# A language-model layer on one core: LSTM cell work placed one or two gate units later, halves kept in pairs, and each step's front begun six units early

## The chip, the core and the metric

One core of a Trainium2 chip. Its engines run their own instruction streams and meet at semaphores: TensorE (PE, matmuls; PEld, its weight loads), VectorE (DVE), ScalarE (ACT), GpSimd (POOL) and SyncE (SP, which here only issues DMAs; ScalarE's queue, ACTq, issues some as well). The metric is the device time of one execution, in microseconds (us).

## What is computed

`x` holds 16 rows of 512 token numbers. For each row:

```
h = concat(emb_table[x], stft_magnitudes(one_hot(x)) @ proj_w + proj_b)    # 512 x 128
h = h + attention(layernorm(h))      # 8 heads of 16; 64 summary tokens, window of 17 keys for the other 448
h = h + moe(layernorm(h))            # 8 experts, top 2
```

The experts of `moe` are LSTMs. The 16 rows are the time steps of the recurrence, the 512 tokens its batch; both choices (K = 2) of all 8 experts carry their own state:

```
gates = xt @ Wi + h @ Wh + b;  i, f, g, o = split(gates, 4)
c = sigmoid(f) * c + sigmoid(i) * tanh(g);  h = sigmoid(o) * tanh(c);  y = h @ Wo + bo
```

with `xt` the token times its 0/1 mask for this choice and expert, and the output the sum over choices of mask x router weight x y.

## The kernel before

Activations lie transposed, 128 features on the partitions and tokens along the free axis; both choices stand side by side, so a gate is 128 x 1024.

**Gate units.** A step s is 32 gate units t = 0..31; expert e = t // 4, gate g = t % 4 in the order I, G, F, O. A unit (`unit_gate`, matmuls on L506) is 12 matmuls of 512 columns: input and hidden state, each split into a high and a low 16-bit half, three products of halves, two choices. It writes one of two PSUM slots, which ScalarE empties with a tanh (`gate_tanh`, L655). Step 0 has no hidden state and no F gate: 24 units of 6 matmuls.

**Cell work.** On VectorE: `masked_input` (L985), `input_part` (L1007), `cell` (L1013, L1017), `hidden` (L992), `hidden_lo` (L997), `chosen` (L1028, L1032: the state of the chosen token's expert, weighted). On ScalarE: `cell_tanh` (L662) and `split_hi` (L666). On TensorE `unit_y` (L512) adds the expert's output. Before the change, counted in units: `cell` at g = 2 of its own expert, `cell_tanh` at g = 3; `hidden` and `split_hi` at g = 0 of the next expert, `hidden_lo` at g = 1, `chosen` at g = 2; `unit_y` at g = 0 of the expert after that.

**The front.** All that a step needs ahead of its LSTM (ids, one-hot, embedding, layernorm, attention, second layernorm, routing, masks) is called the front. The front of step s + 1 is spread by hand over the units of step s: each engine calls `front(t, s + 1)` at unit t, and four tables (`SP_AT`, `PE_AT`, `ACT_AT`, `DVE_AT`) say at which t each piece stands on each engine. Engines run strictly in the order written. Front 0 stands alone ahead of step 0. Pieces that the prediction names, with their lines: embedding matmuls (PE, L420), first transposes (L427), query, key and value (L432), summary scores (L436), window scores (L441, L447: 84 matmuls of 32 columns with block-diagonal weights `diag`), feature scores (L453), values (L459, the same shape), projection (L465, L466), second transposes (L471), logits (L477), mask transposes (L483); on VectorE one-hot (L779), moments (L763 to L789), normalising (L795), value windows (L824), probability transpose (L882); on GpSimd the inverse root (L1105).

**DMAs.** The weights `diag` are filled by four block copies from `pr` (queries, issued by SP) and again by four from `vwin` (values, issued on ScalarE's queue, L619). Routing masks go to DRAM (`mask_scratch`, `mw_scratch`) at t = 28 and come back broadcast: `masks` two for each step's first experts at t = 29, 30, then one per expert; `rowk1` and `roww` at g = 3, each waiting for an earlier `chosen`.

Of the kernel before, what the change touches and what calls it, by code (L numbers as in the profile page):

```python
# [5 lines left out]
def lm_tower_kernel(nc, x_ids, frame_ids, emb_table, proj_w, proj_b, w_qkv, b_qkv, w_out, b_out,  # L6
# [20 lines left out]
    P = 128  # L27
# [43 lines left out]
    with ctx:  # L71
# [16 lines left out]
        tmp = sb("tmp", [P, 7, K * SEQ])  # L88
# [6 lines left out]
        z32 = sb("z32", [P, SEQ])  # L95
# [23 lines left out]
        diag = sb("diag", [P, 2, NBLK, NG, 2 * DH], f16)  # L119
# [14 lines left out]
        qz = pr[:, :].bitcast(f16).rearrange("p (v j c q) -> p v j c q", v=2, j=NBLK, c=2)  # L134
# [3 lines left out]
        vw16 = vwin[:, :].bitcast(f16).rearrange("p (v j d) -> p v j d", v=2, j=NBLK)  # L138
        vhl = ew[:, 0:TF + 2 * PAD].bitcast(f16).rearrange("p (v t) -> p v t", v=2)
# [31 lines left out]
        def gate_at(gate, e):  # L171

            return {I: e % 2, G: 2 + e % 2, F: 4, O: 5 + e % 2}[gate]

        TANH_C = gate_at(F, 0)
# [3 lines left out]
        diag_flat = diag[:, :, :, :, :].rearrange("p v j g d -> p (v j g d)")  # L179
        onehot64 = diag_flat[0:NFFT, 2 * VOCAB * NBJ:3 * VOCAB * NBJ]  # L180
        mag = diag_flat.bitcast(f32)[0:NFREQ, 0:VOCAB * NBJ]
# [100 lines left out]
        def _(sp):  # L282
# [19 lines left out]
            def front(t, b):  # L302
                if t == SP_AT["ids"]:
                    sp_ids(b)
                if t == SP_AT["qbd"]:
# [3 lines left out]
                    for g in range(NG):  # L309
                        load(diag[32 * g:32 * g + 32, :, :, g, :].rearrange("p v j d -> p (v j) d"),  # L310
                             qz[32 * g:32 * g + 32, :, :, :, :].rearrange("p v j c q -> p (v j) (c q)"), S["qbd"])
# [47 lines left out]
            def step(s, par, first, last):  # L359
                for t in range(NG * E):  # L360
                    e, g = t // NG, t % NG
                    if t == 9 and not first:
# [811 lines left out]
```

## Time and profile before

| | |
|---|---|
| median of 3 runs | 1915.93 us (1915.46 to 1918.11) |
| the profiled execution's own time | 1918.11 us, its span 1916.3 us |
| TensorE busy | 1729.1 us (90% of the span) |
| VectorE busy | 1559.5 us (81%) |
| ScalarE busy | 991.9 us (52%) |
| GpSimd busy | 65.2 us (3%) |
| chain that ended last, by engine | PE 40%, DVE 33%, DMA 8%, issue 7%, ACT 5%, ACTq 4% |
| gate matmuls (L506) | 5904, 1451.7 us |

A timeline gives for each instruction its start, its duration, engine, line, operation, what it writes and reads, and in brackets how long its engine was idle before it and what ended the wait. Instructions of one form in a row are merged ("x6"). Matmuls are pipelined, so that one is shown longer than it keeps the next from starting.

### The profile page before, as it was taken

Reading aid. Unit: us, or ns where it says so; the run is one execution under the profiler, and the core shown is the slowest. Engines: PE = TensorE matmul, PEld = TensorE weight load, DVE = VectorE, ACT = ScalarE, POOL = GpSimd, SP = SyncE. Lnnn points to the kernel's source line nnn. Section 1 sums busy time; section 2 is a strip of 40 time slices with the busy share of each in tenths; the row PEclk is TensorE's granted clock in tenths of the full one; section 3 lists DMA queues with packets and bytes.
Section 4 is the critical chain, followed back from the end, with each engine's and each line's share of the span. In section 5 each row is a group of like instructions: output and inputs, shape, how many; then the busy total and the mean of one; then the engine's idle time right before and its main releaser. Section 6 shows DMA issues by size and latency. Waiting matters only on the chain.

```text
span 1916.3 us, 25885 instructions
## 1 busy us (share of the span) xinstructions
PE 1729.1 (90%) x9898; PEld 837.6 (44%) x9898; DVE 1559.5 (81%) x2433; ACT 991.9 (52%) x1114; POOL 65.2 (3%) x42
## 2 busy tenths in 40 slices
PE   3457799999999999999999999999999999999998
PEld 2223344444444444444444444444444444444443
DVE  2649698897988889798898988889898888979865
ACT  3234554646555555645545455455555555564544
POOL 1000000000000000000000000000000000000000
PEclk9668899999999999999999999999999999999999
DMA  3113241413314132232313224151331413223221
GB/s 114 20 41 74 57 67 46 77 37 67 63 49 74 39 70 52 52 70 51 67 45 69 51 57 67 44 80 37 63 66 46 76 37 71 53 50 67 55 61 36
DMA packets 318594, 110.95 MB, mean 58 GB/s; under 512 B 240331, under 2 KB 299581, under 8 KB 318471
## 3 DMA queue, kind: packets, MB, share of 16 engines
q1 hardware_dynamic: 202758, 101.96, 23.9%
q10 hardware_dynamic: 115712, 7.34, 3.8%
q8 instruction: 78, 1.28, 0.3%
q14 instruction: 46, 0.37, 0.1%
HBM read 89.84 MB, written 4.74 MB: 49 GB/s over the span
## 4 chain that ended last, share of the span: by engine, by line
PE 40%; DVE 33%; DMA 8%; issue 7%; ACT 5%; ACTq 4%; SPq 1%; POOL 0%; DVEq 0%
PE gates L506 25%; ACTq L619 4%; DVE C L1017 4%; DVE tmp L1007 4%; DMA masks<-mask_scratch 3%; DVE tmp L1013 3%; DMA prod<-in_x_ids 3%; DVE xm L985 3%; PE yp L512 3%; DVE Hs L997 3%; DVE tmp L1028 3%; DVE xn L795 2%; PE FA L447 2%; ACT tmp L655 2%; PE FA L459 2%
## 5 line engine op out<-in xcount | busy, mean ns | idle before, releaser
L655 ACT ACTIVATE tmp<-gates,bias_sb 128x1024 f32<-128x1024 f32 x504 | 557.5, 1109 | 558.6 <-PE gates L506 496.1
L506 PE MATMUL gates<-xm,wi_sb 128*128 128x512 f16 x3024 | 747.3, 384 | 46.2 <-ACT tmp L655 31.0
L506 PE MATMUL gates<-Hs,wh_sb 128*128 128x512 f16 x2880 | 704.4, 381 | 0.0
L506 PEld LDWEIGHTS gates<-xm,wi_sb 128*128 128x128 f16 x3024 | 290.3, 99 | 435.3 <-issue 105.1
L506 PEld LDWEIGHTS gates<-Hs,wh_sb 128*128 128x128 f16 x2880 | 283.2, 98 | 344.3 <-issue 8.0
L662 ACT ACTIVATE tmp<-C 128x1024 f32<-128x1024 f32 x128 | 135.2, 1057 | 226.4 <-DVE C L1017 223.2
L992 DVE SCALAR_TENSOR_TENSOR tmp<-tmp 128x1024 f32<-128x1024 f32 x128 | 155.9, 1218 | 71.8 <-ACT tmp L662 71.8
L1007 DVE SCALAR_TENSOR_TENSOR tmp<-tmp 128x1024 f32<-128x1024 f32 x120 | 144.9, 1208 | 46.4 <-ACT tmp L655 44.9
L985 DVE TENSOR_TENSOR xm<-xs,masks 128x2048 f16<-128x2048 f16 x128 | 155.2, 1212 | 32.7 <-DMA masks<-mask_scratch 32.7
L997 DVE SCALAR_TENSOR_TENSOR Hs<-tmp,Hs 128x1024 f16<-128x1024 f32 x120 | 146.4, 1220 | 37.7 <-ACT Hs L666 36.7
L1013 DVE SCALAR_TENSOR_TENSOR tmp<-tmp,C 128x1024 f32<-128x1024 f32 x120 | 146.4, 1220 | 14.4 <-ACT tmp L655 14.0
L1017 DVE SCALAR_TENSOR_TENSOR C<-tmp 128x1024 f32<-128x1024 f32 x120 | 147.0, 1225 | 4.1
L666 ACT ACTIVATE Hs<-tmp 128x1024 f16<-128x1024 f32 x120 | 126.5, 1055 | 31.2 <-DVE tmp L992 30.7
L512 PE MATMUL yp<-z,wo_sb 128*128 128x512 f32 x256 | 134.9, 609 | 8.2 <-DVE z L1032 8.2
L1105 POOL TENSOR_TENSOR rstd<-veps,mhalf 128x4 f32<-128x4 f32 x32 | 61.6, 1926 | 1682.6 <-DVE veps L922 1114.8
L1032 DVE TENSOR_TENSOR z<-tmp,roww 128x512 f32<-128x512 f32 x128 | 88.6, 692 | 13.6 <-DVE tmp L1028 0.5
L1028 DVE COPY_PREDICATED tmp<-rowk,tmp 128x512 f32<-128x512 uint16 x128 | 93.0, 727 | 0.1
L512 PEld LDWEIGHTS yp<-z,wo_sb 128*128 128x128 f32 x256 | 48.0, 194 | 38.8 <-issue 12.2
L459 PE MATMUL FA<-vwin,diag 128*128 128x32 f16 x1344 | 36.3, 177 | 7.4 <-DVE vwin L882 7.4
L447 PEld LDWEIGHTS FA<-xn,diag 128*128 128x128 f16 x1344 | 38.2, 97 | 8.1 <-issue 5.5
L459 PEld LDWEIGHTS FA<-vwin,diag 128*128 128x128 f16 x1344 | 36.0, 96 | 12.5 <-DVE vwin L882 9.2
L447 PE MATMUL FA<-xn,diag 128*128 128x32 f16 x1344 | 39.1, 178 | 0.0
(155 smaller groups left out, 1218.9 us busy)
## 6 DMA issues: line engine op xcount, KB each, us to landing
masks<-mask_scratch SPq DMA_DIRECT2D x128, 256.0 KB, 5.0
roww<-mw_scratch SPq DMA_DIRECT2D x128, 256.0 KB, 4.0
rowk<-mask_scratch SPq DMA_DIRECT2D x128, 128.0 KB, 3.0
diag<-pr SPq DMA_DIRECT2D x64, 112.0 KB, 4.3
diag<-vwin ACTq DMA_DIRECT2D x64, 112.0 KB, 4.8
out_dram<-h SPq DMA_DIRECT2D x16, 256.0 KB, 3.7
C<-in_wi SPq DMA_DIRECT2D x1, 2048.0 KB, 10.9
C<-in_wh SPq DMA_DIRECT2D x1, 2048.0 KB, 15.6
```

What stands on the lines that cost most here:

```text
L506: last = mm(gates[:, slot, k * SEQ:(k + 1) * SEQ], w, v, start=(i < K), stop=(i >= len(seq) - K))
L512: mm(yp[:, :], wo_sb[:, e, :], z32[:, :], start=False, stop=(e == E - 1)).then_inc(s_y, 1)
L655: A(tmp[:, gate_at(gate, e), :], gates[:, (n - 1) % 2, :], ACT.Tanh, bias=bias_sb[:, e, gate:gate + 1], scale=UNSCALE).then_inc(s_tanh, 1)
L662: A(tmp[:, TANH_C, :], C[:, e, :], ACT.Tanh, scale=0.5).then_inc(s_tc, 1)
L666: A(Hs[:, e, HI, :], tmp[:, gate_at(O, e), :], ACT.Copy, scale=V_SCALE).then_inc(s_hhi, 1)
L985: TT(xm[:, e % 2, :, :, :], xv, mv_, ALU.mult).then_inc(s_xm, 1)
L992: STT(out=at, in0=at, scalar=1.0, in1=tmp[:, TANH_C, :], op0=ALU.add, op1=ALU.mult).then_inc(s_h, 1)
L997: STT(out=Hs[:, e, LO, :], in0=tmp[:, gate_at(O, e), :], scalar=V_SCALE, in1=Hs[:, e, HI, :], op0=ALU.mult, op1=ALU.subtract).then_inc(s_h ...
L1007: STT(out=at_i, in0=at_i, scalar=1.0, in1=at_g, op0=ALU.add, op1=ALU.mult).then_inc(s_u, 1)
L1013: STT(out=at_f, in0=at_f, scalar=1.0, in1=C[:, e, :], op0=ALU.add, op1=ALU.mult).then_inc(s_v, 1)
L1017: STT(out=C[:, e, :], in0=at_f, scalar=0.5, in1=tmp[:, gate_at(I, e), :], op0=ALU.mult, op1=ALU.add).then_inc(s_c, 1)
L1028: V.copy_predicated(at[:, 0:SEQ], rowk1[:, e % 2, :].bitcast(u16), at[:, SEQ:2 * SEQ]).then_inc(s_sel, 1)
```

## The change

- The tables place each piece of the front again, most of them two units earlier, and the first ones at negative positions -6 to -1, which are units 26 to 31 of the step ahead (`EARLY = 6`, `run_front`). For front 1 these positions come at unit 0 of step 0.
- `cell` moves to g = 0 of the next expert, `cell_tanh` too, `hidden` to its g = 1, `split_hi` to g = 2, `hidden_lo` and `chosen` to g = 3, `unit_y` to g = 1 of the expert after that. F's tanh has two buffers (`tmp` 8 slots instead of 7), and the cell's tanh goes into F's. `chosen` writes into the free half of O's buffer instead of `z32`.
- The two 16-bit halves of queries (`qz`), values (`vp16`) and `diag` lie next to each other in pairs instead of in two planes. The value windows are one 32-bit transpose instead of two 16-bit ones, the block copies move 32-bit pairs (runs of 128 B instead of 64 B), and the weights of window scores and values are read with a step of two elements.
- The embedding matmuls also wait for the mask copies of the front before.

```diff
-    SP_AT = dict(ids=0, qbd=6, rows=28)
-    PE_AT = dict(emb=1, xT=3, qkv=4, summary=7, window=8, feature=14, values=18, proj=21, x2T=23,
-                 logits=24, maskT=27)
-    ACT_AT = dict(h=1, xT=3, qkv=4, split=5, summary=9, window=11, vz=9, pr_hi=15, feature=16, x2T=23,
-                  choice=25, maskT=27)
-    DVE_AT = dict(onehot=0, moments=1, xn=2, pw=5, q_lo=5, kv_lo=6, v_win=7, w_max=8, s_max=9, s_sub=10, w_sum=11,
-                  w_out=12, s_sum=13, s_norm=14, f_max=15, p_lo=16, p_T=16, f_sum=17, f_part=18, attn=19,
-                  moments2=21, xn2=22, x_lo=24, choice1=25, choice2=25, weights=26)
+    SP_AT = dict(ids=-6, qbd=3, rows=28)
+    PE_AT = dict(emb=-3, xT=0, qkv=1, summary=4, window=6, feature=12, values=16, proj=18, x2T=22,
+                 logits=23, maskT=27)
+    ACT_AT = dict(h=-3, xT=0, qkv=1, split=2, summary=6, window=9, vz=7, pr_hi=13, feature=14, x2T=22,
+                  choice=24, maskT=27)
+    DVE_AT = dict(onehot=-4, moments=-2, xn=-1, pw=2, q_lo=2, kv_lo=3, v_win=4, w_max=5, s_max=7, s_sub=8, w_sum=9,
+                  w_out=10, s_sum=11, s_norm=12, f_max=13, p_lo=14, p_T=15, f_sum=16, f_part=16, attn=17,
+                  moments2=19, xn2=20, x_lo=23, choice1=24, choice2=24, weights=25)
+    EARLY = 6
...
+        def run_front(front, t, s):
+            if s == 0 and t == 0:
+                for u in range(-EARLY, 0):
+                    front(u, 1)
+            if s + 1 < STEPS:
+                front(t, s + 1)
+            if s + 2 < STEPS and t >= NG * E - EARLY:
+                front(t - NG * E, s + 2)
...
                 if t == PE_AT["emb"]:
+                    if not is_zero(b):
+                        pe.wait_ge(S["mrow"], b)
+                        pe.wait_ge(S["wT"], b)
...
-                                last = mm(FA[:, r, jj * KB:(jj + 1) * KB], diag[:, qv, j, :, :].rearrange("p g d -> p (g d)"),
+                                last = mm(FA[:, r, jj * KB:(jj + 1) * KB], diag16[:, j, :, qv],
...
-                        act.dma_start(diag[32 * g:32 * g + 32, :, :, g, :].rearrange("p v j d -> p (v j) d"),
-                                      vw16[32 * g:32 * g + 32, :, :, :].rearrange("p v j d -> p (v j) d")) \
+                        act.dma_start(diag[32 * g:32 * g + 32, :, g, :], vwj[32 * g:32 * g + 32, :, :]) \
...
-                    for v in (HI, LO):
-                        own = vhl[:, v, :]
-                        win = bass.AP(tensor=own.tensor, offset=own.offset, ap=[list(own.ap[0]), [QB, NBLK], [1, KB]])
-                        last = V.transpose(vw16[:, v, :, :], win)
-                    last.then_inc(S["vwin"], 1)
+                    win = bass.AP(tensor=vp.tensor, offset=vp.offset, ap=[list(vp.ap[0]), [QB, NBLK], [1, KB]])
+                    V.transpose(vwj, win).then_inc(S["vwin"], 1)
...
             def gate_tanh(s, e, g, first):
-                if gate == F and m >= 1:
-                    act.wait_ge(s_h, m)
+                if gate == F and m >= 2:
+                    act.wait_ge(s_h, m - 1)
                 elif gate == O and m >= 2:
-                    act.wait_ge(s_z, m - 1)
+                    act.wait_ge(s_y, m - 1)
...
             def step(s, par, first, last):          # ScalarE
-                    if g == 3:
-                        cell_tanh(s, e)
+                    if g == 0 and e:
+                        cell_tanh(s, e - 1)
...
-                    if g == 0 and e and not last:
+                    if g == 2 and e and not last:
                         split_hi(s, e - 1)
...
             def step(s, par, first, last):          # VectorE, its order within a unit
+                    if g == 0 and e and not first:
+                        cell(s, e - 1)
                     if g == 1 and e < E - 1:
                         masked_input(s, e + 1, par, first and e == 0)
                     if t == XM_AT and not last:
                         masked_input(s + 1, 0, 1 - par, False)
+                    if g == 3 and e and not last:
+                        hidden_lo(s, e - 1)
+                    if g == 3 and e:
                         chosen(s, e - 1)
                     if t == YADD_AT and not first:
                         add_y(s - 1, 1 - par)
+                    run_front(lambda u, b: front(u, b, b % 2), t, s)
+                    if g == 1 and e:
+                        hidden(s, e - 1)
+                    if g == 2:
                         input_part(s, e, first)
-                    if g == 2 and not first:
-                        cell(s, e)
```

## Rows read from the trace of the kernel before

**Rows 1.** Stretches, length; busy PE, PEld, DVE, ACT, POOL; clock, DMA share, GB/s.

```profile
900.96:1014.89 113.93, 108.22 (x630) 52.44 (x631) 98.06 (x153) 62.06 (x70) 3.82 (x2) 1.00 0.29 58
...
216.71:1812.41 1595.70, 1521.80 (x8821) 737.44 (x8822) 1370.76 (x2127) 862.35 (x965) 53.50 (x28) 0.99 0.29 58
```

**Rows 2.** Timeline of TensorE, step 7; in brackets idle before, and its releaser.

```profile
907.75 1.16 PE L420 MATMUL FB<-table,rows 41*128 41x128 f32 x8 [0.59 <-DVE rows L779]
908.84 1.47 PE L506 MATMUL gates<-xm,wi_sb 128*128 128x512 f16 x6
910.14 1.46 PE L506 MATMUL gates<-Hs,wh_sb 128*128 128x512 f16 x6
...
915.01 0.66 PE L427 MATMUL FB<-ident,xn 128*128 128x128 f32 x4 [0.82 <-DVE xn L795]
...
946.47 1.47 PE L506 MATMUL gates<-xm,wi_sb 128*128 128x512 f16 x6 [0.62 <-ACT tmp L655]
...
966.12 1.47 PE L506 MATMUL gates<-xm,wi_sb 128*128 128x512 f16 x6 [1.47 <-ACT tmp L655]
...
1002.61 0.63 PE L483 MATMUL FB<-ident,pr 128*72 128x128 f32 x4 [1.15 <-DVE pr L973]
...
1014.89 1.46 PE L506 MATMUL gates<-xm,wi_sb 128*128 128x512 f16 x6 [0.44 <-issue]
```

**Rows 3.** Timeline of ScalarE and its queue (ACTq), same step.

```profile
942.40 2.80 ACTq L619 DMA_DIRECT2D diag<-vwin  x2
...
962.96 1.06 ACT L662 ACTIVATE tmp<-C 128x1024 f32<-128x1024 f32 x1 [3.19 <-DVE C L1017]
...
964.98 1.09 ACT L655 ACTIVATE tmp<-gates,bias_sb 128x1024 f32<-128x1024 f32 x1
965.96 1.05 ACT L666 ACTIVATE Hs<-tmp 128x1024 f16<-128x1024 f32 x1
```

**Rows 4.** Timeline of VectorE, same step, a stretch without waits.

```profile
953.30 1.22 DVE L985 TENSOR_TENSOR xm<-xs,masks 128x2048 f16<-128x2048 f16 x1
954.43 1.22 DVE L997 SCALAR_TENSOR_TENSOR Hs<-tmp,Hs 128x1024 f16<-128x1024 f32 x1
...
958.00 0.73 DVE L1028 COPY_PREDICATED tmp<-rowk,tmp 128x512 f32<-128x512 uint16 x1
...
959.45 1.09 DVE L875 TENSOR_TENSOR vwin<-pr,wred 128x896 f32<-128x896 f32 x1
...
966.41 1.11 DVE L882 STREAM_TRANSPOSE vwin<-pr 128x896 f32<-128x896 f32 x1
967.45 1.18 DVE L985 TENSOR_TENSOR xm<-xs,masks 128x2048 f16<-128x2048 f16 x1
```

**Rows 5.** Timeline of all engines and queues, end of the same step.

```profile
1007.15 0.28 SPq L284 DMA_DIRECT2D mw_scratch<-rows  x1
...
1013.57 1.22 DVE L985 TENSOR_TENSOR xm<-xs,masks 128x2048 f16<-128x2048 f16 x1 [1.88 <-DMA masks<-mask_scratch]
```

**Rows 6.** Timeline of VectorE, same step, instructions of the front.

```profile
909.89 0.85 DVE L763 BATCH_NORM_STATS2 stats<-h_sb 128x6 f32<-128x128 f32 x4
...
911.27 1.22 DVE L1007 SCALAR_TENSOR_TENSOR tmp<-tmp 128x1024 f32<-128x1024 f32 x1
...
913.85 1.11 DVE L795 TENSOR_SCALAR xn<-h_sb,mv,rstd 128x128 f32<-128x128 f32 x4
...
932.28 2.10 DVE L824 STREAM_TRANSPOSE vwin<-ew 128x896 f16<-128x896 f16 x2
```

**Rows 7.** Timeline of TensorE, same step, groups without a wait ahead.

```profile
955.11 0.92 PE L453 MATMUL FB<-prod,hones 128*128 128x448 f32 x2
...
961.04 1.02 PE L512 MATMUL yp<-z,wo_sb 128*128 128x512 f32 x2
...
968.72 2.25 PE L459 MATMUL FA<-vwin,diag 128*128 128x32 f16 x84
```

**Rows 8.** Timeline of TensorE, step 0.

```profile
131.93 0.79 PE L427 MATMUL FB<-ident,xn 128*128 128x128 f32 x4 [3.95 <-DVE xn L795]
```

More of the change, by code:

```diff
@@ L361, in step @@
                     e, g = t // NG, t % NG
-                    if t == 9 and not first:
+                    if t == 10 and not first:
                         store(s - 1, 1 - par)
-                    if not last:
-                        front(t, s + 1)
+                    run_front(front, t, s)
                     if g == 1 and e < E - 2:
@@ L373, in step @@
                         rows_in(s + 1, 0)
-            for t in range(NG * E):
+            for t in range(-EARLY, NG * E):
                 front(t, 0)
@@ L540, in step @@
                         y_back(s - 1)
-                    if not last:
-                        front(t, s + 1)
+                    run_front(front, t, s)
             pe.wait_ge(s_const, 16 * len(consts))
@@ L546, in _ @@
             pe.wait_ge(s_prep, 4)
-            for t in range(NG * E):
+            for t in range(-EARLY, NG * E):
                 front(t, 0)
@@ L678, in step @@
                         y_out(s - 1)
-                    if g == 0 and e and not last:
+                    if g == 0 and e:
+                        cell_tanh(s, e - 1)
+                    elif g == 0 and not first:
+                        cell_tanh(s - 1, E - 1)
+                    if g == 2 and e and not last:
                         split_hi(s, e - 1)
-                    elif g == 0 and not e and not first:
+                    elif g == 2 and not e and not first:
                         split_hi(s - 1, E - 1)
-                    if g == 3:
-                        cell_tanh(s, e)
-                    if not last:
-                        front(t, s + 1)
+                    run_front(front, t, s)
             par_of = lambda b: PAR[0]
@@ L706, in _ @@
             split_w_hi(wh_st, wh_sb, 0.5, s_wh_load)
-            for t in range(NG * E):
+            for t in range(-EARLY, NG * E):
                 front(t, 0)
@@ L991, in hidden @@
                 at = tmp[:, gate_at(O, e), :]
-                STT(out=at, in0=at, scalar=1.0, in1=tmp[:, TANH_C, :],
+                STT(out=at, in0=at, scalar=1.0, in1=tmp[:, gate_at(F, e), :],
                     op0=ALU.add, op1=ALU.mult).then_inc(s_h, 1)
@@ L1061, in step @@
                         add_y(s - 1, 1 - par)
-                    if not last:
-                        front(t, s + 1, 1 - par)
-                    if g == 1:
+                    run_front(lambda u, b: front(u, b, b % 2), t, s)
+                    if g == 1 and e:
+                        hidden(s, e - 1)
+                    elif g == 1 and not first:
+                        hidden(s - 1, E - 1)
+                    if g == 2:
                         input_part(s, e, first)
-                    if g == 2 and not first:
-                        cell(s, e)
             dve.wait_ge(s_zero, 1)
-            for t in range(NG * E):
+            for t in range(-EARLY, NG * E):
                 front(t, 0, 0)
@@ L1081, in _ @@
             run_steps(step)
+            cell(STEPS - 1, E - 1)
             hidden(STEPS - 1, E - 1)
@@ L1107, in step @@
             def step(s, par, first, last):
-                if not last:
-                    for t in range(NG * E):
-                        front(t, s + 1)
+                for t in range(NG * E):
+                    run_front(front, t, s)
             pool.wait_ge(s_zero, 1)
-            for t in range(NG * E):
+            for t in range(-EARLY, NG * E):
                 front(t, 0)
```

76 lines of the change are left out of this document (36 added, 40 removed).

## Prediction

> **What bounds the kernel now.** I read the totals by engine first, then the busy sums by step, then TensorE's timeline through one step, and last the timelines of the engines that it waits for. A step is taken from the first gate matmul of one step to that of the next. Fourteen steps (1 to 14) take 1595.70 us, 113.98 each, at a clock of 0.99, which is the 2.4 GHz level; in step 7 VectorE is busy 98.06 of 113.93 us [rows 1]. So neither engine is full. TensorE is the nearer: its matmuls are shown 0.16 us longer than they hold the next one off (half a gate unit is shown as 1.47 us and the next half starts 1.30 us later [rows 2]), and its real idle time is the bracket in a row plus 0.16. Step 7 has seven waits over 0.4 us; their brackets are 0.59, 0.82, 0.62, 1.47, 0.62, 1.15 and 0.44 us (six of the rows stand in [rows 2]), 5.7 in sum, 6.8 with 0.16 each. The rest, 107.1 us, is matmuls back to back: that is the floor of a step, and 6.8 to 6.9 us a step (14 x 6.9 = 97 us) is all that another order can win.
>
> What each wait hangs on: embedding matmuls on the one-hot rows (0.59), the first transposes on the normalised input (0.82), gate units on a tanh of ScalarE (0.62 and 1.47), the second transposes (0.62), the mask transposes (1.15), the step's first gate unit on the masked input (0.44) [rows 2]. Behind the 0.62 one stands ScalarE's queue issuing the value copies, of which two took 2.80 us [rows 3]; behind the 1.47 one ScalarE waited 3.19 us for VectorE's new cell state before it could go on to the next gates [rows 3].
>
> **The change part by part.** Positions are gate units t of a step, four to an expert.
>
> *Cell work later.* Nothing is removed; cell, hidden, its halves and the chosen row move one or two positions later, and F's tanh gets a second buffer. ScalarE's tanh of the cell now comes after the next expert's first gate. From G's tanh to that point are three units, 7.8 us; VectorE must fit in input part, low half, chosen row and cell: 1.14 + 1.14 + 1.45 + 2.4 = 6.1 us (an operation over 1024 elements lets the next begin 1.13 to 1.14 us later, the chosen row's two take 1.45, and the cell is two long ones, the second waiting for the first) [rows 4], and the gates' two PSUM slots give ScalarE 1.9 us more (two units, 5.2, less the cell's tanh, the gate tanh ahead of it and the one behind, 1.1 each [rows 3]). So 3.6 us of front work fits in the last two positions of an expert. By the ops' durations the experts have 0 to 3.2 us there; only the last has more, and there TensorE waits in any case (below). The 1.47 wait and the 0.62 behind the value copies go: there the queue's four issues now come at t = 7, before units with 1.9 us of bias and output matmuls among them. I take these as won, worth 1.63 + 0.78.
>
> *Front begun six units early.* Ids are asked for at t = 26 of the step before the last one; SP's queue reaches it right after the row loads of t = 23, five units (13 us) before the one-hot, so the ids wait goes (0.75). The embedding's new wait for the mask copies is for copies made two units earlier, at no cost while those stand. The second transposes (t = 22, statistics at 19) and mask transposes (t = 27, weights at 25) get two units and one unit more and lose their waits (0.78 and 1.31). The mask copies no longer queue behind the cell's tanh, so the masked input is ready before the step's first unit (0.59).
>
> *What is late next, first place: the first transposes.* The moments at t = 30 stand on VectorE's queue behind the next step's masked input, and that waits for a load of masks. Counted from the end of unit 27: VectorE ends chosen row at +2.3 (ScalarE's tanh and high half of unit 26 end at -0.4, then 1.14 + 1.45), SP's row loads that wait for it take 0.8, the mask rows go out at +3.4, and from there to the masked input's start are 6.42 us in the row, 1013.57 - 1007.15 [rows 5]: +9.8. Then masked input 1.14, moments 1.38, input part 1.14, low half 1.14, chosen row 1.45, normalising 1.11 [rows 4, 6]: +17.2. The 1.9 us of GpSimd between the moments and the normalising lie beside the three in the middle. TensorE comes there after the mask transposes 0.47, five units 12.95, output matmuls 0.86 and embedding 1.09 [rows 2, 7]: +15.4. Wait: 1.8 us, where 0.98 was.
>
> *Second place: the values.* They need the transposed probabilities, now at t = 15 for t = 16. VectorE is held at t = 11 for the high half, 2.25 us after unit 10 (a tanh 0.2 after the unit, 0.98 to the next start, 1.05 [rows 3]). From there it is never free: the stretch from the masked input at 953.30 to 967.45, fifteen instructions back to back, is the same list less one low half and one chosen row [rows 4]: 14.15 + 1.14 + 1.45 = 16.7. TensorE needs six units 15.54, feature scores 0.76, output 0.86 [rows 7] = 17.2. Wait: 2.25 + 16.7 + 0.05 - 17.2 = 1.9 us, where none was shown.
>
> *Halves in pairs.* Two 16-bit transposes of 2.10 us together [rows 6] become one of 32 bits on the same 896 elements; the existing one of that form takes 1.11 [rows 4], so VectorE gains 1.0 us a step, beside the path but for the first front. The block copies move runs of twice the length and half as many; at worst they cost what they do (2.80 us for two [rows 3]), at best half. The strided writes of ScalarE may cost 0.1 to 0.3 us a step; all but the first front's lie where both engines have room. The diagonal weights are now read with a gap between elements. Today 84 such loads with their 32-column matmuls take 2.25 - 0.16 = 2.1 us, 25 ns a pair [rows 7]. Bounds: 25 ns as now, or, if a load gets only one column in the time in which a 512-column matmul streams one (216 ns / 512 x 128), 54 ns. I take 25, since the second matmul group already streams paired halves at the price of the first; that is the moving side, though, so 54 stays as a rival.
>
> The rule that bears on this: the Trainium skill, "TensorE: Matmul & The Clock Gate", section on weight-path perf modes, says that the fast load takes 128 columns of a type other than fp32, packed or strided, but also that it reads 32 bits at a time, two 16-bit weights. By its first half the pair costs what it does, and the sum would be 1872. By its second a gap could waste half of each read; an estimate from that page, at twice the time for a pair, is 15 x 168 x 25 ns = 63 us more, 1935. The trace of before has no such load, so it shows neither.
>
> *Ends of the run.* In step 0 the early six positions of front 1 fall behind its first unit. There the chain is bare: today the transposes come at 131.93 after a wait of 3.95 us [rows 8]. They now start some 2.6 us sooner by the clock but with two units fewer behind them (5.2 us); I take +2, bounds -3 and +7. The first front, a bare chain, loses 1.0 of transpose and perhaps as much of copying: -2. The tail keeps its chain (the last cell still starts when F's tanh is there): 0.
>
> **Sum.** A step: 107.1 + 1.8 + 1.9 = 110.8 to 110.9 against 113.98, 3.1 less; 14 steps: -43.5; ends 0. The profiled execution took 1918.11 us with a span of 1916.3, so 1874.6; the median of the runs, 1915.93, gives 1872.4. I say 1872.
>
> **The rivals.**
> *All waits gone.* If the mask load lands a microsecond or two sooner and VectorE's list is shorter than counted, a step falls to 107.1 and the run to 1915.9 - 97 = 1819. For it: both waits left are under 2 us. Against: they are two separate chains, each counted from rows. Chance 0.10, most of it only part of the way.
> *The waits move, and nothing is won.* VectorE with 97 us of work and some 1.5 us of gaps in 111 is 89% full; if it reaches each cell more than the 3.6 us late, ScalarE holds the gates again. It takes 0.4 us at each of eight experts to eat the 3.1: 1916. For it: no spare time from t = 11 to 16. Against: elsewhere it is held for ScalarE's high half, so it has time. Chance 0.15, of it 0.06 still faster, 0.05 within 0.2% and 0.04 slower.
> *Slower: the spaced weights.* At 54 ns a pair, 168 pairs a step cost 4.9 us more, all on TensorE, whose floor they raise, in the 15 fronts that lie inside steps: 15 x 4.9 = 73, so 1872 + 73 = 1945. It decides from 3.1 us / 168 = 18 ns on, 43 ns a pair. Chance 0.11.
>
> **The numbers.** The forecast has 0.64; its own range is 1855 to 1893 (1.3 us a step either way, and 5 us at the ends). Faster by over 0.2% (about what a measurement of this kernel can tell from no change): 0.64 + 0.10 + 0.06 = 0.80. Within: 0.05. Slower: 0.04 + 0.11 = 0.15. The range goes to 1848 below (part of "all gone") and 1908 above (part of "nothing won"), leaving out the spaced weights and the rest.
>
> **What the profile after would show.** Right: steps of about 111 us; no wait over 0.4 us at the embedding, second transposes, mask transposes and step's first unit; one of 1.6 to 1.8 (bracket) at the first transposes, released by the normalising, and one like it at the values, released by the 32-bit transpose; gate units with no wait for ScalarE; groups of 42 diagonal matmuls in 1.05 us as today. Wrong, if those groups take over 1.8 us, if the cell's tanh shows waits of several microseconds followed by idle gates, or if masks land later than 10 us after unit 27.

## The result and the profile after

The changed kernel takes 1947.24 us (median of 4 runs, 1944.00 to 1949.43) against 1917.02 for the kernel before in the same runs: ratio 1.0156, 95% interval 1.0137 to 1.0174. It is slower; the forecast of 1872 and its range are missed. The profiled execution took 1947.46 us, its span is 1945.7.

The page of the changed kernel: totals of the engines, and the value copies with their us from issue to landing.

```profile
PE 1740.4 (89%) x9898; PEld 850.1 (44%) x9898; DVE 1548.8 (80%) x2417; ACT 998.0 (51%) x1114; POOL 63.4 (3%) x42
...
diag<-vwin ACTq DMA_DIRECT2D x64, 112.0 KB, 7.5
```

Stretches of the changed kernel (columns as in [rows 1]): step 8, steps 1 to 14, step 0.

```profile
1026.01:1142.11 116.10, 109.16 (x630) 53.38 (x631) 97.39 (x152) 62.00 (x70) 3.82 (x2) 0.99 0.26 57
212.56:1841.81 1629.25, 1533.98 (x8812) 748.77 (x8813) 1360.63 (x2112) 870.38 (x965) 53.52 (x28) 0.98 0.26 57
...
116.42:212.56 96.14, 67.59 (x390) 32.55 (x391) 71.45 (x128) 50.32 (x59) 2.01 (x2) 0.82 0.29 63
```

Steps 1 to 14 take 116.37 us each where they took 113.98 [rows 1]: 33.5 us in all. The start is shorter, step 0 beginning at 116.42 instead of 120.16, and step 0 itself takes 96.14. TensorE's timeline in step 8 and at its end:

```profile
1026.01 1.46 PE L522 MATMUL gates<-xm,wi_sb 128*128 128x512 f16 x6 [0.60 <-issue]
...
1032.21 0.90 PE L443 MATMUL FB<-ident,xn 128*128 128x128 f32 x4 [3.45 <-DVE xn L811]
1032.90 2.77 PE L522 MATMUL gates<-xm,wi_sb 128*128 128x512 f16 x6
1035.46 1.68 PE L522 MATMUL gates<-Hs,wh_sb 128*128 128x512 f16 x6
...
1055.71 1.21 PE L463 MATMUL FA<-xn,diag 128*128 128x32 f16 x42
...
1069.20 1.04 PE L522 MATMUL gates<-xm,wi_sb 128*128 128x512 f16 x4 [1.16 <-ACT tmp L669]
...
1091.05 1.11 PE L475 MATMUL FA<-vwin,diag 128*128 128x32 f16 x38 [1.93 <-DVE vwin L895]
...
1113.65 0.60 PE L487 MATMUL FB<-ident,xn 128*128 128x128 f32 x4
...
1128.70 0.60 PE L499 MATMUL FB<-ident,pr 128*72 128x128 f32 x4
...
1135.27 1.16 PE L436 MATMUL FB<-table,rows 41*128 41x128 f32 x8
...
1142.11 1.46 PE L522 MATMUL gates<-xm,wi_sb 128*128 128x512 f16 x6 [0.40 <-issue]
```

Of the waits of [rows 2], those at the embedding, the second transposes and the mask transposes are gone (1135.27, 1113.65, 1128.70), and so is the 1.47 behind the cell's tanh. In their place stand 3.45 us at the first transposes, 1.16 at the gate unit after t = 9 (0 to 1.5 over the steps), 1.93 at the values and 0.40 (0.4 to 1.8 over the steps) at the step's first unit. And half a gate unit, which starts the next half 1.30 us later [rows 2], takes 2.56 right behind the first transposes (1032.90 to 1035.46): the clock is granted at 1.2 GHz for 3.41 us.

The clock's record counts 19 such stretches of 3.41 us begun in steps 1 to 14, where before had 5, and 4.1 us of a longer one that began in step 0. Of the 19, 13 begin behind the first transposes, 4 behind the values and 2 behind the wait after t = 9. If half of each stretch is lost, a step loses 2.46 us to the clock, and 0.61 before. By this count a step at full clock takes 113.91, and 113.37 before: the rest grew by 0.5 us a step, the clock's loss by 1.9. The experiments are read in the same three numbers.

The count is an upper bound for the clock, because other engines catch up while TensorE is slow, and waits that follow get shorter (in E9 below the gate unit after t = 9 waits 0.36 us in step 9, which has a stretch, and 1.11 in step 10, which has none). TensorE's timeline gives another split: its idle time (each bracket over 0.15 us plus 0.16) is 7.4 us a step, 6.3 before, and its matmuls, at whichever clock, fill 108.9, and 107.7 before. **So waits and clock share the 2.4 us a step about evenly: 1.15 and 1.25.**

### The profile page after: what moved, and what is told of

The parts are those of the page before. It is cut to its first block, busy times and chain, and to the rows that moved or that the text cites. A ratio compares the mean times of both kernels' runs of the same rounds, so it can differ in the third digit from the quotient of the medians.

```text
span 1945.7 us, 25741 instructions
## 1 busy us (share of the span) xinstructions
PE 1740.4 (89%) x9898; PEld 850.1 (44%) x9898; DVE 1548.8 (80%) x2417; ACT 998.0 (51%) x1114; POOL 63.4 (3%) x42
## 4 chain that ended last, share of the span: by engine, by line
PE 56%; DVE 25%; DMA 7%; ACTq 5%; issue 4%; ACT 3%; SPq 1%; POOL 0%; DVEq 0%
PE gates L522 40%; ACTq L634 5%; DVE Hs L1010 3%; DMA masks<-mask_scratch 3%; PE yp L528 3%; DVE xm L998 3%; DMA mw_scratch<-rows 2%; DVE tmp L1020 2%; DVE tmp L1041 2%; PE FA L475 2%; DVE tmp L1005 2%; PE FA L463 2%; PE FA L448 1%; PE FB L482 1%; ACT tmp L669 1%
## 5 line engine op out<-in xcount | busy, mean ns | idle before, releaser
L522 PE MATMUL gates<-xm,wi_sb 128*128 128x512 f16 x3024 | 763.5, 390 | 41.2 <-issue 15.1
L522 PEld LDWEIGHTS gates<-xm,wi_sb 128*128 128x128 f16 x3024 | 295.1, 100 | 444.8 <-issue 129.6
L528 PE MATMUL yp<-tmp,wo_sb 128*128 128x512 f32 x256 | 134.0, 605 | 5.9 <-DVE tmp L1043 5.9
L1043 DVE TENSOR_TENSOR tmp<-tmp,roww 128x512 f32<-128x512 f32 x128 | 88.6, 692 | 4.4
L817 DVE TENSOR_TENSOR prod<-qT,kw 128x64 f32<-128x64 f32 x16 | 4.4, 275 | 83.9 <-ACT kf L613 83.9
L443 PE MATMUL FB<-ident,xn 128*128 128x128 f32 x64 | 16.0, 397 | 60.7 <-DVE xn L811 60.7
L528 PEld LDWEIGHTS yp<-tmp,wo_sb 128*128 128x128 f32 x256 | 47.8, 193 | 36.0 <-issue 12.7
```

The source lines that it names most:

```text
L522: last = mm(gates[:, slot, k * SEQ:(k + 1) * SEQ], w, v, start=(i < K), stop=(i >= len(seq) - K))
L528: mm(yp[:, :], wo_sb[:, e, :], chosen_at(e), start=False, stop=(e == E - 1)).then_inc(s_y, 1)
```

## The experiments

"Step" is the mean length of steps 1 to 14, "clock" half of the time that it spent at the half clock, "rest" the difference; "clock" is an upper bound, so that "rest" is somewhat too low where "clock" is large. Step, clock and rest are those of the profiled execution. Medians stand against 1917 to 1920 us of the kernel before on the same chip.

| kernel | us | ratio, 95% interval | step | clock | rest |
|---|---|---|---|---|---|
| before | 1917.0 | | 113.98 | 0.61 | 113.37 |
| after | 1947.2 | 1.0156 (1.0137 to 1.0174) | 116.37 | 2.46 | 113.91 |
| E1 mask rows at 27 | 1890.2 | 0.9851 (0.9833 to 0.9869) | 112.57 | 1.58 | 110.99 |
| E2 store at 14 | 1960.5 | 1.0198 (1.0175 to 1.0220) | 117.35 | 3.29 | 114.06 |
| E3 pairs alone | 1896.0 | 0.9875 (0.9861 to 0.9890) | 112.86 | 0.37 | 112.49 |
| E4 later cell alone | 1997.7 | 1.0394 (1.0367 to 1.0422) | 119.24 | 5.40 | 113.84 |
| E5 early front alone | 1949.3 | 1.0161 (1.0146 to 1.0176) | 115.54 | 3.69 | 111.85 |
| E6 value copies at 6 | 1944.7 | 1.0131 (1.0116 to 1.0146) | 116.28 | 3.61 | 112.67 |
| E7 rows 27, values 17 | 1847.7 | 0.9625 (0.9609 to 0.9642) | 109.50 | 0.37 | 109.14 |
| E8 E7 and copies at 6 | 1840.3 | 0.9593 (0.9579 to 0.9608) | 108.95 | 0.85 | 108.09 |
| E9 values 17 alone | 1917.7 | 0.9993 (0.9981 to 1.0004) | 114.18 | 1.96 | 112.22 |
| E10 moments first | 1931.0 | 1.0062 (1.0047 to 1.0077) | 115.18 | 2.71 | 112.47 |
| E11 E8, moments first | 1831.7 | 0.9546 (0.9532 to 0.9560) | 108.43 | 0.69 | 107.74 |
| E12 E4, rows at 27 | 1942.7 | 1.0132 (1.0102 to 1.0161) | 115.32 | 3.53 | 111.79 |
| E13 waits filled | 1943.5 | 1.0114 (1.0093 to 1.0135) | 115.90 | 1.10 | 114.79 |
| E14 E6, filled | 1925.3 | 1.0034 (1.0021 to 1.0046) | 114.88 | 1.08 | 113.80 |
| E15 E11, filled | 1834.1 | 0.9553 (0.9539 to 0.9567) | 108.61 | 0.81 | 107.80 |
| E16 E11, one bias matmul | 1816.8 | 0.9465 (0.9448 to 0.9482) | 107.50 | 0.12 | 107.38 |
| E17 E13, one bias matmul | 1921.5 | 1.0004 (0.9992 to 1.0017) | 114.09 | 0.26 | 113.83 |

### The parts of the change, each alone (E3, E4, E5)

E3 is the kernel before with the pairs: `diag`, `qz`, `vp16` interleaved, one 32-bit transpose, 32-bit copies, weights read with a step. E4 is the kernel before with the cell work of the changed one. E5 is the kernel before with the changed tables and `run_front`.

> The kernel before with the halves in pairs and nothing else. Theory (pairs cost nothing, weights with a step of two load as fast): 84 diagonal matmuls in 2.1 us as before, value copies issued in 3 us instead of 4.4, the 0.6 to 0.8 us wait for ScalarE behind them gone; 1900 to 1912 us. Rival (pair runs slow the copies on ScalarE's queue): four issues of 6 us or more, 1925 us or above.

> The kernel before with the cell work later (second buffer of F, orders of ScalarE, VectorE and TensorE within an expert) and nothing else: the old tables, planes instead of pairs. Theory (the later cell takes the wait of 1.47 us for ScalarE away and brings none): 1.5 us a step less, 1890 to 1900 us. Rival (work moved past the front's pieces makes the front late, and the waits at transposes grow by as much): 1912 us or more.

> The kernel before with the new tables, the front begun six units early and the embedding's new wait, and nothing else: old cell order, planes instead of pairs. Theory (the late mask load is made by the chosen row and SP's row loads being later, so with the old cell order the mask rows go out without row loads ahead of them): write to masked input in 6.5 us as before, wait at the first transposes 1 us or less, total 1885 to 1905 us. Rival (the early front itself makes the chain masks, moments, normalising too long): first transposes wait over 3 us and the clock falls behind it, 1925 us or more.

The pairs win 24 us, more than was expected: the value copies issue in 3.0 us instead of 4.4, landing after 3.1 instead of 4.8, and the start is 3.6 us shorter. ScalarE's writes with a gap take longer, 0.77 us instead of 0.66 for each of two and 0.73 instead of 0.59 for one, 0.36 us a step. From the page of E3:

```profile
diag<-vwin ACTq DMA_DIRECT2D x64, 112.0 KB, 3.1
```

The other two lose, so both rivals had the time right, but neither had the place. In E5 the mask load is issued 1.45 us after the second write, as before, and the masked input starts 5.9 to 6.6 us after that write: this half of the theory came true. The rest falls by 1.5 us a step (1.7 to 2.3 us of wait at the first transposes, 3.08 at the values, at most 1.0 elsewhere), but the clock takes 3.1 more, nearly all of it behind the values and behind the projection, and step 0 takes 104.6 instead of 96.6. In E4 the waits grow not at transposes but in three other places, at the embedding (1.1 to 3.3), the values (1.76) and the step's first unit (1.8 to 3.4), and the clock takes 4.8 more.

### The mask rows behind the row loads (E1, E12)

```diff
-    SP_AT = dict(ids=-6, qbd=3, rows=28)
+    SP_AT = dict(ids=-6, qbd=3, rows=27)
```

> The changed kernel with the mask rows written to DRAM at t = 27, ahead of SP's two row loads, instead of at t = 28 behind them. Theory (the mask load is late because its writes stand behind the row loads, and take 3.4 us there instead of 1.5): the masked input of the next step starts 2.5 to 3 us sooner, the wait at the first transposes falls from 3.45 to under 1.2 us, the wait at the step's first gate unit goes, and TensorE's clock stays at its upper level there; 1865 to 1885 us. Rival 1 (VectorE's own list between masked input and normalising is too long whatever the load does): the 3.45 stays, about 1947 us. Rival 2 (the clock falls at any wait there): the wait shrinks but the clock share stays 0.985 in every step, about 1895 to 1900 us.

> The kernel before with the later cell work alone (1997.7), and the mask rows written at t = 27 instead of 28. Theory A: the later chosen row holds SP's row loads back and the mask rows stand behind them, which makes the wait of 2 to 3.4 us at each step's first unit; it falls under 1 us, 25 to 40 us less in all, 1955 to 1975, the waits at embedding and values staying. Rival: the step's first unit waits for the cell work itself, and moving the rows does nothing: 1990 to 2000.

The changed kernel between unit 27 and the transposes that wait, ScalarE, VectorE and SP's queue:

```profile
1130.51 0.59 ACT L656 ACTIVATE rows<-FB 8x512 f32<-8x512 f32 x1
1130.93 0.69 DVE L1043 TENSOR_TENSOR tmp<-tmp,roww 128x512 f32<-128x512 f32 x1
...
1131.65 0.35 SPq L362 DMA_DIRECT2D rowk<-mask_scratch  x1
...
1132.04 0.42 SPq L364 DMA_DIRECT2D roww<-mw_scratch  x1
1132.59 0.35 SPq L298 DMA_DIRECT2D mask_scratch<-ew  x1
...
1132.98 0.32 SPq L298 DMA_DIRECT2D mw_scratch<-rows  x1
...
1136.34 1.19 SPq L352 DMA_DIRECT2D masks<-mask_scratch  x2
...
1140.79 1.22 DVE L998 TENSOR_TENSOR xm<-xs,masks 128x2048 f16<-128x2048 f16 x1 [4.42 <-DMA masks<-mask_scratch]
...
1147.15 1.11 DVE L811 TENSOR_SCALAR xn<-h_sb,mv,rstd 128x128 f32<-128x128 f32 x4
```

The rows are ready at 1131.1, yet go out at 1132.59 and 1132.98, behind two row loads that had to wait for the chosen row (1131.6). SP issues the mask load only once both writes have landed, 3.36 us after the second. The same place in E1:

```profile
1098.95 0.31 SPq L298 DMA_DIRECT2D mask_scratch<-ew  x1
...
1099.56 0.27 SPq L298 DMA_DIRECT2D mw_scratch<-rows  x1
1100.10 0.35 SPq L362 DMA_DIRECT2D rowk<-mask_scratch  x1
1100.49 0.42 SPq L364 DMA_DIRECT2D roww<-mw_scratch  x1
1101.03 1.17 SPq L352 DMA_DIRECT2D masks<-mask_scratch  x2
...
1105.99 1.23 DVE L998 TENSOR_TENSOR xm<-xs,masks 128x2048 f16<-128x2048 f16 x1 [1.18 <-DMA masks<-mask_scratch]
```

The second write has landed by 1101.03, after 1.47 us at most. So a write right behind two loads lands 1.9 us later than one ahead of them. The Trainium skill, "DMA: Bandwidth & Descriptors", section on queues, rings and completion order, says that a DMA's semaphore is counted only after every earlier write of the same DMA engine, across its queues. The trace agrees as far as it goes: all of the writes' semaphore counts but one come at 1135.54 to 1136.32, those of the two loads until 1136.16. It does not tell whether the writes' data, too, stood behind the loads' in the queue. In E1 the wait at the first transposes is 0.8 to 2.0 us, the one at the step's first unit is gone, and 57 us come off, 5 less than the least that was expected. No low stretch is left behind the first transposes from step 2 on, but one now follows the values in 12 of 14 steps, where 4 had one in the changed kernel with the same pause of 1.93 us. E12 shows the same on the cell work alone: the wait at the first unit goes, and 55 us with it, more than expected, up to half of it clock. In E4 these rows made that wait:

```profile
1166.33 0.32 SPq L360 DMA_DIRECT2D rowk<-mask_scratch  x1
...
1167.23 0.38 SPq L296 DMA_DIRECT2D mask_scratch<-ew  x1
...
1170.97 0.90 SPq L350 DMA_DIRECT2D masks<-mask_scratch  x2
...
1175.51 1.23 DVE L997 TENSOR_TENSOR xm<-xs,masks 128x2048 f16<-128x2048 f16 x1 [4.46 <-DMA masks<-mask_scratch]
1176.84 1.58 PE L517 MATMUL gates<-xm,wi_sb 128*128 128x512 f16 x6 [2.47 <-issue]
```

### The value copies on ScalarE's queue (E2, E6)

The changed kernel, ScalarE and both queues at t = 9 and 10:

```profile
1060.19 0.32 SPq L362 DMA_DIRECT2D rowk<-mask_scratch  x1
...
1060.86 7.07 ACTq L634 DMA_DIRECT2D diag<-vwin  x4
1061.09 0.38 SPq L352 DMA_DIRECT2D masks<-mask_scratch  x1
1061.56 0.41 SPq L370 DMA_DIRECT2D out_dram<-h  x1
...
1068.03 1.11 ACT L669 ACTIVATE tmp<-gates,bias_sb 128x1024 f32<-128x1024 f32 x1 [6.12 <-issue]
```

Four issues hold ScalarE for 7.07 us and the next tanh with it. E2 moves the store away from them (`if t == 14 and not first:` instead of 10), E6 the copies away from the loads (`vz=6` instead of 7 in `ACT_AT`).

> The changed kernel with the output store at t = 14 instead of t = 10, so that its 256 KB do not meet the value block copies of ScalarE's queue. Theory A (the store slows the four issues from 4.4 to 6.7 us and so holds the gate tanh): the four issues take 4.5 us or less, the wait of 0.5 to 1.5 us at the gate unit after t = 9 goes, 1931 to 1937 us. Theory B (the mask and row loads that leave at the same moment do it): issues stay at 6 us or more, 1945 to 1949 us. Theory C (runs of 128 bytes do it): as B, and the kernel before with pairs shows it too.

> The changed kernel with the value block copies at t = 6 of ScalarE's queue instead of t = 7, so that they are issued before SP's mask and row loads of the first chosen row leave. Theory (these loads, at the same moment, stretch the four issues to 6.7 us): four issues in 3 to 3.5 us, as with pairs alone, and no wait of 0.5 to 1.5 us at the gate unit behind t = 9; 1930 to 1936 us. Rival (the copies are slow after any late position, or the wait has another releaser): issues over 6 us or the wait stays, 1945 us or more.

E2 is 13 us slower instead of faster, of which the clock column has 12, and the issues still take 5.9 to 7.3 us. In E6 they start 1.9 us before SP's loads instead of among them:

```profile
1059.22 3.31 ACTq L634 DMA_DIRECT2D diag<-vwin  x4
1061.16 0.32 SPq L362 DMA_DIRECT2D rowk<-mask_scratch  x1
```

Over the steps from 2 on they take 3.0 to 3.4 us. So here it is the loads, not the store. (In E5, with the old 64 B runs, the copies leave 0.5 us behind the store and 2.6 behind a mask load and take 5.2 to 7.0, so that a store may do it too; no run separates the two there.) The wait after t = 9 is gone and the rest falls by 1.24 us a step, which is the 17 us that were expected; the clock takes 1.15 more, with a stretch behind both pauses in nearly every step, and 2.5 us are left of it.

### The values a unit later (E7, E8, E9)

```diff
-    PE_AT = dict(emb=-3, xT=0, qkv=1, summary=4, window=6, feature=12, values=16, proj=18, x2T=22,
+    PE_AT = dict(emb=-3, xT=0, qkv=1, summary=4, window=6, feature=12, values=17, proj=19, x2T=22,
...
-                  w_out=10, s_sum=11, s_norm=12, f_max=13, p_lo=14, p_T=15, f_sum=16, f_part=16, attn=17,
-                  moments2=19, xn2=20, x_lo=23, choice1=24, choice2=24, weights=25)
+                  w_out=10, s_sum=11, s_norm=12, f_max=13, p_lo=14, p_T=15, f_sum=16, f_part=16, attn=18,
+                  moments2=20, xn2=21, x_lo=23, choice1=24, choice2=24, weights=25)
```

E9 has this edit alone, E7 with E1's, E8 with E1's and E6's.

> The changed kernel with mask rows written at t = 27 and with the values one unit later (TensorE t = 17, what follows them one later as well). Theory (the wait of 1.93 us at the values is VectorE's list from t = 11 to 15, and the 3.4 us at the clock's lower level that follow it in every step are its consequence): the wait falls under 0.4 us, the lower level goes from the steps, 3.6 us a step less than with the rows alone: 1838 to 1850 us. Rival 1 (the clock falls without the wait too): 1862 us. Rival 2 (the wait moves on to the attention sum and projection): 1880 us or more.

> The changed kernel with all three: mask rows at t = 27, value copies at t = 6, values at t = 17. If the three causes are separate, their gains add: about 1 us a step less than with the first and third alone, 1825 to 1838 us. If one wait merely takes the place of another, it ends within 5 us of the kernel without the copies moved.

> The changed kernel with only the values and what follows them one unit later, the mask rows left at t = 28. Both theories: the wait of 1.93 us at the values goes (14 x 2.1 = 29 us), the one of 3.45 at the first transposes stays. Theory A, the long wait by itself brings TensorE's clock down for 3.41 us in each step: clock about 0.985, time 1903 to 1920. Rival, the clock only falls because a step has two long waits: clock 0.995 or more, time 1898 or less.

E7 and E9 came out as expected (E9 by theory A), E8 2 us above: against E7 its rest falls by 1.05 us a step and the clock takes 0.48 back. Alone the edit wins 30 us, beside E1's 43, because there the fall of the clock behind the values goes with it (17 us in the clock column, 7 in E9). But E9 also shows the limit of theory A, for the clock falls behind the first transposes in 9 of 14 steps only. Steps 9 and 10 of the same run, their stretches first, then TensorE in them:

```profile
1129.12:1242.84 113.72, 108.77 (x631) 53.54 (x632) 97.41 (x152) 62.53 (x70) 3.83 (x2) 0.98 0.26 58
1242.84:1355.54 112.70, 107.43 (x630) 52.80 (x631) 97.39 (x152) 61.59 (x70) 3.83 (x2) 1.00 0.29 58
```

```profile
1135.32 1.12 PE L443 MATMUL FB<-ident,xn 128*128 128x128 f32 x4 [3.45 <-DVE xn L811]
1136.23 2.29 PE L522 MATMUL gates<-xm,wi_sb 128*128 128x512 f16 x5
```

```profile
1249.04 0.66 PE L443 MATMUL FB<-ident,xn 128*128 128x128 f32 x4 [3.46 <-DVE xn L811]
1249.54 1.46 PE L522 MATMUL gates<-xm,wi_sb 128*128 128x512 f16 x6
```

The same pause of 3.45 us brings the clock down in one step and not in the next.

### The order of moments and masked input (E10, E11)

```diff
-                    if t == XM_AT and not last:
-                        masked_input(s + 1, 0, 1 - par, False)
...
                     run_front(lambda u, b: front(u, b, b % 2), t, s)
+                    if t == XM_AT and not last:
+                        masked_input(s + 1, 0, 1 - par, False)
```

> The changed kernel with one order reversed: at t = 30 VectorE does the early front's moments ahead of the next step's masked input instead of behind it. Theory A, the moments' 1.38 us fit in the 4.4 us in which VectorE waits for the mask load, so that the normalising and the first transposes come 1.4 us earlier and nothing else later: wait 3.45 to about 2.0, 1926 to 1930, or 1903 to 1915 if the clock no longer falls there. Rival, the step's start then waits for the masked input instead: 1942 to 1950.

> The kernel with mask rows at t = 27, value copies at 6 and values at 17 (1840.3), with the moments ahead of the masked input. Theory A: the last wait, 0.83 to 1.8 us at the first transposes, goes, 14 x 1.25 = 17 us, or 27 with the clock's low stretches: 1812 to 1825. Rival: the mask load now lands before the moments are over, so the masked input comes late for the step's first unit, and the wait only moves: 1835 to 1842.

In E10 the wait at the first transposes is 2.06 us in every step, 1.4 less, and the masked input starts only 0.3 us later after the second write (8.3 us on the mean instead of 8.1): theory A's mechanism, and 16 us instead of 17 to 21. The clock still falls, in most steps twice. E11 wins 9 us, half of the 17: 0.82 us of the wait stay in every step, now behind ScalarE's high half, then VectorE's low half, chosen row and normalising, a chain that the moments are no part of.

### Pauses filled with matmuls (E13, E14, E15)

```diff
+                    for _i in range(0 if is_zero(b) else 15):
+                        mm(FB[:, :], wi_sb[:, 0, HI, 0:P], wi_sb[:, 0, LO, 0:4 * P], start=True, stop=True)
...
+                    pe.wait_ge(S["df"], b1)
+                    for _i in range(0 if is_zero(b) else 8):
+                        mm(FB[:, :], wi_sb[:, 0, HI, 0:P], wi_sb[:, 0, LO, 0:4 * P], start=True, stop=True)
```

The 15 stand ahead of the wait at the first transposes, the 8 ahead of the one at the values. E13 is the changed kernel with both, E14 is E6 with both, E15 is E11 with 4 at the first place alone.

> The changed kernel with extra matmuls of 512 columns whose results nobody reads, 15 (3.2 us) ahead of the wait at the first transposes and 8 (1.7 us) ahead of the one at the values. They fill the pauses and take no work away, so the waits' time stays spent. Theory A, TensorE's pauses bring its clock down and that costs 2.46 us a step: the clock in steps 1 to 14 stays at 1.00, and the time falls by about 14 x 2.4 = 34 us: 1910 to 1920. Rival, the clock falls for another reason (the work itself, its 16-bit columns): it falls as before or more, 1943 to 1955.

> The changed kernel with the value copies issued at unit 6 (1944.7) and the same fillers in both pauses. Theory A, the 1.2 us a step that the earlier copies won there were lost to a second fall of the clock in each step (3.61 us a step in all): 1944.7 - 14 x 3.6 = 1894, 1890 to 1902. Rival, the earlier copies win nothing: same as the kernel with fillers alone, 1910 to 1920, or 1943 and more if fillers do nothing.

> The fastest kernel so far (1831.7: mask rows at 27, value copies at 6, values at 17, moments ahead of the masked input), with 4 fillers (0.86 us) ahead of its one wait of 0.82 us. Theory A: the clock's four low stretches in steps 1 to 14 (0.69 us a step) go, 1822 to 1828. Rival: they follow the chain of small matmuls later in the step and stay, 1830 to 1836.

TensorE in E13, step 8:

```profile
1033.05 3.40 PE L442 MATMUL FB<-wi_sb 128*128 128x512 f16 x15
1036.68 0.66 PE L445 MATMUL FB<-ident,xn 128*128 128x128 f32 x4 [0.22 <-DVE xn L816]
1037.18 1.46 PE L527 MATMUL gates<-xm,wi_sb 128*128 128x512 f16 x6
```

From step 2 on not one low stretch is left behind the first transposes or behind the values, in E13 or E14: the pauses had brought the clock down. Eight are left in each, all 73 to 75 us into a step. The sum came out far from the expectation, 3.8 us instead of 34 in E13 and 19 instead of 50 in E14. In E13 the clock column gives 19 of the 34, since the eight stay. The rest takes 12 back: TensorE, no longer slowed, waits longer for the masked input at the step's start (0.7 to 2.2 us, 0.3 more on the mean), and the loss by the clock had been counted too high. And step 0 takes 100.4 us instead of 96.2. E14 against E13 is 18 us, near the 17 that the earlier copies were worth in the rest of E6, but in the profiled executions 6 us of the difference lie in step 0. E15 wins nothing (2.4 us more, where the rival had it).

### The projection's small matmuls (E16, E17)

The eight stretches begin where the projection ends, 3.1 to 3.8 us after its first matmul. In the kernel before it is the same: four of its five (steps 1, 6, 9 and 12) begin 3.5 to 3.7 us after the projection's first matmul. TensorE in E15:

```profile
713.15 0.39 PE L483 MATMUL FB<-wout_sb,attn 128*128 128x128 f32 x2
...
715.96 0.48 PE L484 MATMUL FB<-bout_sb,ones 1*128 1x128 f32 x2
716.38 2.60 PE L524 MATMUL gates<-xm,wi_sb 128*128 128x512 f16 x6
```

```diff
-                    for i in range(TILES):
-                        mm(FB[:, i * D:(i + 1) * D], attn[:, i * P:(i + 1) * P], wout_sb[:, :], start=True, stop=False)
-                        last = mm(FB[:, i * D:(i + 1) * D], ones1[:, :], bout_sb[:, :], start=False, stop=True)
+                    mm(FB[:, :], ones1[:, :], bout_sb[:, :].rearrange("p (a d) -> p a d", a=1).to_broadcast([1, TILES, D]),
+                       start=True, stop=False, skip_group_check=True)
+                    for i in range(TILES):
+                        last = mm(FB[:, i * D:(i + 1) * D], attn[:, i * P:(i + 1) * P], wout_sb[:, :],
+                                  start=False, stop=(i == TILES - 1), skip_group_check=True)
```

> The fastest kernel (1831.7), with the projection's bias added by one matmul of 512 columns ahead of the four products, instead of one of 128 columns behind each: four of 0.42 us become one of about 0.85, 0.84 us a step less work on TensorE. Theory A, the clock's last low stretches follow the projection because its group of eight small matmuls lasts 3.2 us; with 2.5 us they go: 14 x (0.84 + 0.69) = 21 us less, 1808 to 1814. Rival, they follow for another reason and stay: only the work is saved, 1817 to 1822.

> The changed kernel with its two pauses filled (1943.5), and the same one bias matmul. Theory A: the eight stretches left in steps 1 to 14, all behind the projection, go; steps fall by 0.84 + 0.7 on the mean, part of it given back as a longer wait for the masked input at the step's start: 1921 to 1932. Rival, they stay: 1932 to 1940.

TensorE in E16:

```profile
706.18 1.12 PE L480 MATMUL FB<-bout_sb,ones 1*128 1x512 f32 x2
707.23 1.16 PE L483 MATMUL FB<-wout_sb,attn 128*128 128x128 f32 x8
708.22 1.46 PE L524 MATMUL gates<-xm,wi_sb 128*128 128x512 f16 x6
```

The group takes 2.04 us instead of 3.23, and the stretches are gone: steps 2 to 14 of E16 run at full clock throughout, and E17 has one stretch left in its profiled execution. E16's 14.9 us lie between the two theories (0.4 us of the saving turned up as a wait at the second transposes in each step); its clock decides for A. E17 is at 1921.5, at A's lower edge (its profiled execution was 7.6 us below its median and had a mean granted clock of 0.977, most of the others 0.972 to 0.975, so that the median run will hold a few more stretches). E16, at 1816.8 us, is the fastest version: 5.3% less than before.

## Why the prediction was wrong

**The floor and the waits that go: right.** E11 has steps of 107.9 us at full clock with one wait of 0.82; less 0.98 that is 106.9, and the floor was put at 107.1. The waits at embedding, second and mask transposes and behind the cell's tanh went in the changed kernel as said. The prologue won 3.7 us, where 2 was said; step 0 lost nothing, where 2 was said.

**Pairs: right.** 42 pairs take 1.21 us as before: 25 ns with a gap between the weights. The rival of 54 ns is out. The Trainium skill, "TensorE: Matmul & The Clock Gate", section on weight-path perf modes, has the fast load read its weights "packed or strided"; the trace agrees, with 25 ns a pair at either spacing. The 32-bit transpose takes 1.10. ScalarE's strided writes cost 0.36 us a step, where 0.1 to 0.3 was said.

**Values: right in size.** 1.9 us of idle time was said, a bracket of 1.7; the bracket is 1.93, so 2.1.

**First transposes: the step that failed in the sum of waits.** "The mask rows go out at +3.4, and from there to the masked input's start are 6.42 us": the second write goes out at +4.28 (1132.98 less 1128.70), and from there to the masked input are 7.81 us. Of the first 0.9 us, 0.6 come from VectorE, whose chosen row ends at +2.9 (1130.93 + 0.69 less 1128.70) and not at +2.3. The other 1.4 come from SP's queue: the mask load is issued 3.36 us after the second write, where in before it was 1.46. I had seen that the row loads stand ahead of the mask rows and charged 0.8 us of issue, but not that a write behind loads lands later; in before the chosen row was one unit earlier and the loads had left 5 us ahead of the write, so its 6.42 did not hold here. The masked input starts at +12.1, not +9.8, the normalising ends at +19.6, not +17.2, and the wait is a bracket of 3.45 us, 3.6 of idle time, not 1.8. The same 2.3 us make the wait at the step's first unit, which I had called gone. E1 and E12 undo SP's part with one number. The mask load of before, to set beside the second write at 1007.15 in [rows 5]:

```profile
1008.61 0.90 SPq L338 DMA_DIRECT2D masks<-mask_scratch  x2
```

**The copies' issue: the second step that failed, a bound too low.** "At worst they cost what they do": the four take 7.07 us, not twice 2.80, because they now leave with SP's loads; that is the 1.16 us at the gate unit (0.75 on the mean of the steps), which I took as won. E6 shows it.

**The clock: the third, a term missing from the sum.** I read 0.99 in [rows 1] and went on as if it were 1, though 1% of 114 us was there to be asked about. My two waits were priced at their length alone. A step of the forecast had 3.7 us in two pauses; the real one has 3.6 and 2.1, and the steps have 14 low stretches more, 17 of the 19 right behind the two. E13 and E14 show that pauses caused them. What a stretch adds to its step differs: 1.2 us in E13 (116.3 against 115.1), 1.4 in E9 (113.7 to 114.3 against 112.3 to 112.7), but 1.7 in E11 (109.6 against 107.9), where no later wait is left to take it up. By the split of the timeline above the clock made 17.5 us and the waits 16 of the 33.5 that the steps lost; by the plain count the clock made 26.

Added up, a step: 110.9 said; on the mean 1.7 more at the first transposes, 0.2 at the values, 0.9 after t = 9, 1.0 at the step's start and 1.8 of clock (108.9 of matmuls less the floor of 107.1) give 116.5; 116.37 it is.

What stays open: why the same pause is followed by the low clock in one step and not in the next (E9; the values in E1 and in the changed kernel), and so what a pause costs before it is tried.

## What to carry to other kernels

A step moved to another slot takes its neighbours on every queue with it: read off what its DMAs will leave beside and behind, since landing and issue times measured elsewhere do not hold there. On TensorE price a pause (here of 1.2 us and more), and also a long group of small matmuls, at its length and up to 1.7 us of low clock, and look at the granted clock step by step before trusting a sum of waits. When a large reordering disappoints, its parts may still be good: three moves in the tables (the mask rows, the value copies, and the values with what follows them) turned 1947 into 1840.

## What the runs showed of the hardware

- A small write to DRAM was waited for 1.47 us when issued ahead of two broadcast loads and 3.36 right behind them.
- Four copies of 128 B runs issued from ScalarE's queue took 3.0 to 3.4 us when SP issued nothing or issued its loads 1.9 us later (E3, E6), and 6.0 to 7.5 when they left right behind SP's loads (the changed kernel).
- TensorE fell to 1.2 GHz for 3.41 us behind pauses of 1.9 and 3.5 us (once each also of 1.2 and 1.5), though not each time, and behind eight fp32 matmuls of 128 columns in 3.23 us without any pause, in 8 of 14 steps of E13 and 4 of the kernel before; with the same product in 2.04 us it did so in no step of E16 and none of the profiled E17.
- The mean step was 116.37 us in the changed kernel and 116.28 in E6, with 7.4 and 6.8 us of idle time: the clock took back what the edit had won.
- ScalarE's 16-bit writes with a gap of one element took 0.77 us instead of 0.66 for 448 elements and 0.73 instead of 0.59 for 464 (E3 and before).
